# Score masks added by VectorE, softmax sums inverted in packed form and spread by way of DRAM

## What is computed

```python
B, S, D = (2, 512, 512)           # x has shape (2, 512, 512)
NH, NKV = (32, 8); HD = D // NH   # 32 heads of 16, 8 key/value groups of 4 heads each
q, k, v = x @ wq, x @ wk, x @ wv
scores = einsum('bihd,bjhd->bhij', q, k) * HD ** -0.5
scores = where(causal, scores, finfo.min)
attn = softmax(scores, axis=-1)
out = einsum('bhij,bjhd->bihd', attn, v).reshape(b, s, NH * HD) @ wo
```

## Time and profile before

| | us |
|---|---|
| median of 3 runs | 952.16 |
| range of the runs | 950.35 to 952.4 |
| the profiled execution | 952.0 |
| its span in the profile | 950.1 |
| attention stage in it | about 84 to 289 |

### The profile page before, as it was taken

How to read it: one execution, slowest core, us unless ns; L and a number is a source line. 1 busy time by engine, 2 the same in 40 slices (tenths; PEclk the granted TensorE clock), 3 DMA queues, 4 the chain that set the end, 5 groups by cost and what they waited for, 6 DMA issues and landing times.

```text
span 950.1 us, 13799 instructions
## 1 busy us (share of the span) xinstructions
PE 877.9 (92%) x5224; PEld 693.3 (73%) x5224; DVE 693.6 (73%) x892; ACT 533.1 (56%) x707; POOL 189.5 (20%) x197
## 2 busy tenths in 40 slices
PE   2799999999988889898999999999988999999996
PEld 1567667666667668686888888788866888888885
DVE  3835698888888768778677777587887866667842
ACT  3313667657654434486666657477727766666830
POOL 3002555666557213300000000000040000000004
PEclk9798999999898999999999999999999999999998
DMA  9588565655535103105233333133312333332202
GB/s 309 171 243 152 67 109 69 113 101 66 103 78 179 34 12 105 51 22 147 83 106 103 102 99 113 46 105 95 111 45 67 111 104 97 99 101 67 67 1 89
DMA packets 40610, 93.59 MB, mean 99 GB/s; under 512 B 7000, under 2 KB 10072, under 8 KB 40544
## 3 DMA queue, kind: packets, MB, share of 16 engines
q1 hardware_dynamic: 36416, 87.35, 36.6%
q10 hardware_dynamic: 4128, 5.36, 1.7%
HBM read 77.98 MB, written 2.11 MB: 84 GB/s over the span
## 4 chain that ended last, share of the span: by engine, by line
PE 75%; DVE 9%; issue 5%; POOL 4%; ACT 3%; DMA 2%; SPq 1%; POOLq 0%; DVEq 0%; ACTq 0%
PE PS L1509 15%; PE PS L1510 14%; PE PS L1511 14%; PE PS L1815 5%; PE PS L1814 5%; PE PS L1813 5%; PE PS L1607 4%; PE PS L1639 2%; PE PS L1622 2%; DVE MX L1295 2%; POOL QS L731 2%; DMA WM<-in_WM 1%; POOL X L715 1%; PE PS L1531 1%; DVE ACC L1157 1%
## 5 line engine op out<-in xcount | busy, mean ns | idle before, releaser
L837 ACT ACTIVATE PL<-CODE 128x1024 f32<-128x1024 int32 x200 | 201.9, 1057 | 60.3 <-DVE ACC L1157 55.7
L1509 PE MATMUL PS<-HH,WRH 128*128 128x512 f32 x448 | 176.7, 394 | 11.2 <-DVE HL L1116 4.7
L1510 PE MATMUL PS<-HH,WRL 128*128 128x512 f32 x448 | 175.6, 392 | 0.0
L1511 PE MATMUL PS<-HL,WRH 128*128 128x512 f32 x448 | 175.6, 392 | 0.0
L715 POOL TENSOR_TENSOR X<-X,SCR 128x512 f32<-128x512 f32 x32 | 42.6, 1343 | 560.2 <-DVE SCR L1142 560.1
L1157 DVE SCALAR_TENSOR_TENSOR ACC<-PL,ACC 128x1024 f32<-128x1024 f32 x100 | 123.1, 1231 | 8.4
L879 ACT ACTIVATE PT<-PS 128x512 f32<-128x512 f32 x160 | 85.5, 602 | 67.3 <-PE PS L1622 45.1
L1295 DVE TENSOR_REDUCE MX<-PS 128x2 f32<-128x256 f32 (+3 forms) x128 | 100.5, 820 | 29.4 <-PE PS L1609 14.8
L1509 PEld LDWEIGHTS PS<-HH,WRH 128*128 128x128 f32 x448 | 84.9, 189 | 31.2 <-issue 6.3
L731 POOL TENSOR_TENSOR QS<-ident,MX 64x256 fp32r<-64x256 f32 x128 | 93.6, 732 | 66.6 <-DVE MX L1295 60.0
L1511 PEld LDWEIGHTS PS<-HL,WRH 128*128 128x128 f32 x448 | 84.8, 189 | 18.0
(11 more groups left out here) (225 smaller groups left out, 1528.2 us busy)
## 6 DMA issues: line engine op xcount, KB each, us to landing
CODE<-in_CODES SPq DMA_DIRECT2D x50, 512.0 KB, 3.5
SCALE<-in_SCALES SPq DMA_DIRECT2D x100, 256.0 KB, 4.0
WM<-in_WM SPq DMA_DIRECT2D x12, 1024.0 KB, 5.9
QS<-FH SPq DMA_DIRECT2D x32, 128.0 KB, 4.1
QS<-FL SPq DMA_DIRECT2D x32, 128.0 KB, 5.1
X<-in_X ACTq DMA_DIRECT2D x2, 1024.0 KB, 12.3
GAB<-gates SPq DMA_DIRECT2D x4, 512.0 KB, 3.8
out_x<-X ACTq DMA_DIRECT2D x8, 256.0 KB, 2.0
```

The lines of the kernel that those rows point to most:

```text
L837: nc.scalar.activation(PL[:, n % 3], CODE[:, p % 2], ACT.Prelu, scale=scale, bias=bias, alpha=alpha).then_inc(s_plane, 1)
L1509: nc.tensor.matmul(dst, lh, rh, start=start and k == 0, stop=False)
L1510: nc.tensor.matmul(dst, ll, rh, start=False, stop=False)
L1511: ins = nc.tensor.matmul(dst, lh, rl, start=False, stop=stop and k == KC - 1)
```

## The change

- `scores(n)` no longer adds the mask by a product. DVE reads each head's scores and a mask CMASK (three blocks of zeros and the triangular block, so that its last (ic + 1) x 128 columns fit every unit), adds them, writes the sum back over the scores, and takes the maximum in the same instruction: four `tensor_tensor_reduce` a unit in place of two `reduce_max`. The transposed scores keep their mask product. POOL writes CMASK once before unit 0.
- For pairs 0 to 5 the shuffle and the two reciprocals are gone. SP packs the sums of a pair (two DMAs, from 4 rows of 512 to 64 rows of 32 each) into RC, DVE inverts RC (128x32) at u = 7, SP stores it to DRAM (two DMAs) with odd and even group exchanged, and spreads it over the 128 partitions of DENS (one DMA, 2 KB each). The division comes at u = 16 for pairs 0 to 4, at unit 61 for pair 5; before, it came at u = 9. Pair 6 is swapped, inverted and divided as before, in units 61 to 63; pair 7 after the loop as before.
- The packs of pair c stand on SP's queue ahead of stack 2c + 5, the stores ahead of stack 2c + 6 (pair 5's behind stack 15), the spread behind stack 2c + 6 (pair 5's behind stack 15).
- `step_at` uses slots 0, 1, 5 of eight units in place of 2, 4, 6. `ROUND_AT` moves pair 5 from unit 60 to 62.

```diff
--- before.py
+++ after.py
@@ -78,12 +78,16 @@
 
 LOW_RANK_AT = [(0, KC - 1), (1, 1), (1, KC - 1)]
 PAIRS = GROUPS // 2
-ROUND_AT = {41: 0, 46: 1, 49: 2, 54: 3, 58: 4, 60: 5, 63: 6}
+ROUND_AT = {41: 0, 46: 1, 49: 2, 54: 3, 58: 4, 62: 5, 63: 6}
 SPLIT_AT = {46: 0, 51: 1, 54: 2, 59: 3}
 SWAP = list(range(HD, 2 * HD)) + list(range(HD))
 
 
 STEPS = len(CAPS) + 1
+
+
+PACK_AT = {2 * pair + 5: pair for pair in range(B * PAIRS - 2)}
+SPREAD_AT = {min(2 * pair + 6, B * GROUPS - 1): pair for pair in range(B * PAIRS - 2)}
 
 
 SECOND_AT = 2
@@ -115,7 +119,7 @@
 
 def step_at(n):
 
-    slots = (2, 4, 6)
+    slots = (0, 1, 5)
     if not 0 <= n < B * GROUPS * TB or n % 8 not in slots:
         return None
     return divmod(n // 8 * len(slots) + slots.index(n % 8), STEPS)
@@ -247,6 +251,8 @@
         MR = sb("MR", [P, D], F32)
         gab0 = at[0]
         GAB = sb("GAB", [P, B, D], F32)
+        CMASK = sb("CMASK", [P, TB * P], F32, gab0)
+        RC = sb("RC", [P, S // HD], F32, gab0 + 4 * TB * P)
         MCOL = sb("MCOL", [P, 2, 4, KC, B], F32)
         ident = sb("ident", [P, P], F32)
         maskR = sb("maskR", [P, P], F32R)
@@ -359,6 +365,7 @@
         XN = [sb(f"XN{n}", [P, TB, D], F32, R0 + off * K) for n, off in enumerate((40, 40, 40, 40))]
         XM = [sb(f"XM{n}", [P, 2, D], F32, R0 + off * K) for n, off in enumerate((72, 16, 80, 48))]
 
+        INV = nc.dram_tensor("inverses", (REP, 2, S), F32, kind="Internal").ap()
         GD = nc.dram_tensor("gates", (4, B, D), F32, kind="Internal").ap()
 
         PS = ctx.enter_context(nc.psum_tensor("PS", [P, 8, 512], F32))
@@ -432,6 +439,10 @@
         s_pl = sem("projection_weights_split")
         s_ll = sem("lora_weights_split")
         s_gd = sem("gates_stored")
+        s_dn = sem("denominators_packed")
+        s_ri = sem("denominators_inverted")
+        s_rs = sem("inverses_stored")
+        s_rb = sem("inverses_spread")
         s_gab = sem("gates_spread")
         s_sg = sem("silu_ready")
         s_hsh = sem("hidden_rounded")
@@ -535,6 +546,31 @@
                 sp.wait_ge(s_free, J[last_gated(i - 1)] + 1)
             sp.wait_ge(s_gd, 16 * B)
             sp.dma_start(GAB[:], GD[i:i + 1].to_broadcast([P, B, D])).then_inc(s_gab, 16)
+
+        def pack_sums(sp, pair):
+
+            b, c = divmod(pair, PAIRS)
+            sp.wait_ge(s_odd, 2 * pair + 2)
+            if pair:
+                sp.wait_ge(s_rs, 32 * pair)
+            for u in range(2):
+                sp.dma_start(RC[64 * u:64 * u + 64], DEN[HD * u:P:2 * HD, c, b * S:(b + 1) * S]).then_inc(s_dn, 16)
+
+        def store_inverses(sp, pair):
+
+            sp.wait_ge(s_ri, pair + 1)
+            if pair:
+                sp.wait_ge(s_rb, 16 * pair)
+            for u in range(2):
+                sp.dma_start(INV[:, 1 - u], RC[64 * u:64 * u + 64]).then_inc(s_rs, 16)
+
+        def spread_inverses(sp, pair):
+
+            sp.wait_ge(s_rs, 32 * (pair + 1))
+            if pair:
+                sp.wait_ge(s_div, pair)
+            sp.dma_start(DENS[:], INV.rearrange("h u s -> (h u) s").unsqueeze(1).to_broadcast([GROUPS, HD, S])
+                         ).then_inc(s_rb, 16)
 
         def load_stack(sp, n):
 
@@ -621,7 +657,15 @@
                                  ).then_inc(s_wm[n % 3], 16)
 
             for n in range(B * GROUPS):
+                if n in PACK_AT:
+                    pack_sums(sp, PACK_AT[n])
+                if n - 1 in PACK_AT:
+                    store_inverses(sp, PACK_AT[n - 1])
                 load_stack(sp, n)
+                if n == B * GROUPS - 1:
+                    store_inverses(sp, PACK_AT[n])
+                if n in SPREAD_AT:
+                    spread_inverses(sp, SPREAD_AT[n])
                 if n == STACKS:
                     sp.wait_ge(s_mr, 1)
                     for b in range(B):
@@ -674,6 +718,11 @@
             pool.wait_ge(s_free, J["norm", 0, B - 1, KC - 1] + 1)
             for odd in range(2):
                 link(nc.gpsimd.memset(V[:, :, odd::2, 1 - odd, :], 1.0))
+            pool.wait_ge(s_mm, J["modcol", 1, COLS[-1]] + 1)
+            pool.wait_ge(s_const, 16 * 3)
+            link(nc.gpsimd.memset(CMASK[:, 0:(TB - 1) * P], 0.0))
+            nc.gpsimd.tensor_copy(CMASK[:, (TB - 1) * P:], maskB[:]).then_inc(s_ones, 1)
+            pool.wait_ge(s_ones, 3)
             pool.wait_ge(s_mm, J["v", B - 1] + 1)
             for i in range(1, STACKS):
                 link(nc.gpsimd.memset(KN[i][64:P].bitcast(F32), -1.0))
@@ -1226,8 +1275,14 @@
                 cols = slice(half * (S // 2), (half + 1) * (S // 2))
                 link(nc.vector.reciprocal(DENS[:, cols], DENS[:, cols]))
 
+            def invert_packed(pair):
+                dve.wait_ge(s_dn, 32 * (pair + 1))
+                nc.vector.reciprocal(RC[:], RC[:]).then_inc(s_ri, 1)
+
             def divide(pair):
                 b, c = divmod(pair, PAIRS)
+                if pair < B * PAIRS - 2:
+                    dve.wait_ge(s_rb, 16 * (pair + 1))
                 cols = slice(b * S, (b + 1) * S)
                 nc.vector.tensor_tensor(NUM[:, c, cols], NUM[:, c, cols], DENS[:], ALU.mult).then_inc(s_div, 1)
                 dve.wait_ge(s_div, pair + 1)
@@ -1292,21 +1347,30 @@
                     if n >= 2:
                         dve.wait_ge(s_dg, 2 * (n - 1))
                     w = (n % TB + 1) * P
-                    nc.vector.reduce_max(MX[:, n % 2, 2 * pair:2 * pair + 2], PS[:, 2 * pair:2 * pair + 2, 0:w], AX_X
-                                         ).then_inc(s_mx, 1)
+                    if n == 0:
+                        dve.wait_ge(s_ones, 3)
+                    for h in (2 * pair, 2 * pair + 1):
+                        ins = nc.vector.tensor_tensor_reduce(PS[:, h, 0:w], PS[:, h, 0:w], CMASK[:, TB * P - w:], 1.0,
+                                                             MASKED, ALU.add, ALU.max, MX[:, n % 2, h:h + 1])
+                    ins.then_inc(s_mx, 1)
                 if step_at(n) and step_at(n)[1] < STEPS - 1:
                     curve_sum(*step_at(n))
                 if n == TB - 1:
                     gate_values()
                 if pair_at(n, 4) is not None:
                     copy_odd(pair_at(n, 4))
-                if pair_at(n, 5) is not None:
-                    swap_sums(pair_at(n, 5))
-                for half, unit in enumerate((5, 6) if n >= 60 else (7, 8)):
-                    if pair_at(n, unit) is not None:
-                        invert(half)
-                if pair_at(n, 7 if n >= 60 else 9) is not None:
-                    divide(pair_at(n, 7 if n >= 60 else 9))
+                if pair_at(n, 7) in PACK_AT.values():
+                    invert_packed(pair_at(n, 7))
+                if pair_at(n, 16) in range(B * PAIRS - 3):
+                    divide(pair_at(n, 16))
+                if n == B * GROUPS * TB - 3:
+                    divide(B * PAIRS - 3)
+                    swap_sums(B * PAIRS - 2)
+                    invert(0)
+                if n == B * GROUPS * TB - 2:
+                    invert(1)
+                if n == B * GROUPS * TB - 1:
+                    divide(B * PAIRS - 2)
                 if n in SPLIT_AT:
                     split_heads(SPLIT_AT[n])
 
@@ -1604,10 +1668,8 @@
                     if n >= 1:
                         pe.wait_ge(s_mx, 2 * (n - 1) + half + 1)
                     for h in (2 * half, 2 * half + 1):
-                        nc.tensor.matmul(PS[:, h, 0:(ic + 1) * P], QS[:, q % STACKS, h, ic * P:(ic + 1) * P],
+                        ins = nc.tensor.matmul(PS[:, h, 0:(ic + 1) * P], QS[:, q % STACKS, h, ic * P:(ic + 1) * P],
                                          KS[:, q % STACKS, 0:(ic + 1) * P], start=True, stop=True)
-                        ins = nc.tensor.matmul(PS[:, h, ic * P:(ic + 1) * P], identR, maskR[:], start=False, stop=True,
-                                               skip_group_check=True)
                     ins.then_inc(s_s, 1)
 
             def transposed(n):
```

## The result

Median of the change 979.11 us (973.26 to 980.22, 4 runs), beside it the kernel before at 952.28: ratio 1.0271, 95% interval 1.0226 to 1.0316. The profiled execution took 978.4 us, its span is 976.6. So the change costs 26 us where 14 were forecast. The busy times on the page after, which answer to the earlier trace rows: PE has 11.0 us less, DVE 1.6 less, and still the kernel is slower.

The account below looks back on a forecast made before the run. In the attention stage PE and DVE were both nearly full and waited for each other. From 952.0 us, adding 0 (PE against DVE), 7.4 (moved decode steps), 3.4 (clock) and 3.0 (SP's queue) gave 966 us; range 944 to 984.

Parts of the forecast that it names:

- its own case: Whole kernel: the forecast of 966 us, 960 to 974, given a chance of 0.42.
- dear maxima: Rival on DVE: each delivered maximum costs 0.177 instead of 0.07 us, half of 27 us exposed, 980 us; chance 0.17.
- Term B: Moved decode steps: ACT waits for codes of piece 4 (4.5 us) and longer for piece 5; +7.4 us, bounds +4 and +12.
- term C: Granted clock: PE slows after the new wait for piece 4's codes; +3.4 us, bounds 0 and 7.
- Term A: PE against DVE in attention: PE loses 18.6 us of masks, DVE gains 3.6 net; taken as 0, bounds -18.6 and +15.
- Term D: SP's queue: five more DMAs for each of six pairs use up its idle time; +3 us, bounds 0 and +18.
- Faster: Rival in attention: cheap maxima, fewer reciprocals and PE's relief win; the stage gains 8 us at most, 944 us; chance 0.20.
- Queue and clock hold: Rival: SP's queue absorbs its added DMAs and the clock holds; 959 us (954 to 960); chance 0.17.
- the signs named beforehand: Profile after: two ACT code waits of 4 to 8 us, lower clock, maxima 0.533 plus 0.14 to 0.2 us, groups near 11.4.

Follow-up runs that it names:

- e6: Kernel before with only the codes of pieces 2 to 5 issued ahead of the stack loads: 949.9 us, ratio 0.9964.
- e7: Kernel before with packed softmax sums and early codes; masks stay on PE, slots 2, 4, 6: 950.5 us, ratio 0.9981.
- e8: The whole change, but with decode slots 2, 4, 6 and early codes: 951.9 us, ratio 1.0019.
- e2: The change with its new slots, but the codes of pieces 2 to 5 issued ahead of the stack loads: 960.8 us, ratio 1.0098.
- e4: Kernel before with only the masks of the first scores moved from PE to DVE: 959.0 us, ratio 1.0072.
- e1: The change with the decode slots put back to 2, 4, 6, nothing else different: 959.5 us, ratio 1.0082.
- e3: Kernel before with only the decode slots moved to 0, 1, 5: 979.0 us, ratio 1.0284.
- e9: Kernel before with decode slots 0, 1, 5 and early codes: 964.9 us, ratio 1.0123.
- e12: Kernel before with packed sums, decode slots 0, 1, 5 and early codes; masks stay on PE: 963.4 us, ratio 1.0140.
- e10: Kernel before without the mask products in the first scores and nothing in their place: 947.2 us, ratio 0.9962.
- e5: Kernel before with only the softmax sums packed; masks on PE, slots 2, 4, 6, late codes: 957.3 us, ratio 1.0053.
- e11: Kernel before with packed sums, early codes, old slots and no mask in the first scores: 951.3 us, ratio 0.9997.

## Why the prediction was right or wrong

**The direction and the wide range (944 to 984) held; the forecast was 13 us too low, and the 960 to 974 given for its own case were missed by 5.** That the time lies inside the range is in part luck: the range reached so far up for dear maxima, whose 980 is next to the 979 measured, and the maxima were not dear.

One chain of runs in which each step changes one thing adds up to the 25.8 us (each step to some 3 us, the last to some 5): from the kernel before to e6 (early codes) -3.4, to e7 (sums) +1.6, to e8 (masks) +3.6, to e2 (slots) +7.5, to the change (late codes) +16.5. So late codes cost 13.1 more than they did before, where B and C had 10.8; the masks 3.6, where A had 0; the sums 1.6, where D had 3; and the place of the slots 7.5, which no term had. This last one is the largest miss. Another order gives other shares: masks 6.9 (e4), sums on top 0.9 (e1 less e4), slots with the codes that they make late 18.0.

**Term B (+7.4) and term C (+3.4): right mechanism, somewhat too small.** The two waits came at exactly the two places named, 6.64 and 8.05 us in place of 4.5 and 4.4 to 5. Without the packed sums they were 4.43 and 3.94 (e3), so the sum behind B holds for the slots alone. The step that failed is that issue and landing were taken at the times of the trace before. Piece 4's codes were to be issued 0.43 us after ACT's last exponential; behind a spread, a pack and eleven us of stack it became 2.5, and 2.5 + 4.16 is the 6.64. Piece 5's came 1.1 us after it, as forecast, but took 7.0 us from issue to use instead of 4.05, right behind a spread. The clock was counted with one new wait, at 3.4 us. Counted in the same way, 10 us x (1 - granted clock), the four windows shown give 1.3 + 3.8 + 4.1 + 2.7 = 11.9 us, of which the kernel before already had 3.4: an upper bound, since PE stood idle for part of them. The runs measure both terms together: early codes take 16.5 us from the change and 3.4 from the kernel before, and the 13.1 between them stand against 10.8.

**What the prediction did not have: where the slots lie.** It followed the moved steps for their codes only. That 5 and 8 = 5 + 3 are both slots, so that curves and a fold meet behind the copy of the even group in one unit of ACT, could be read from `ride(n + 3)` and `step_at`. It costs 7.5 us in the change and 15.1 on the kernel before (e9 less e6). In one group 6.5 us of it are shown for the masked kernels (e2, e8) and 5.1 for e12; the rest stays open.

**Term A (0): too small by 3 to 7 us.** Masks cost 6.9 us alone (e4), 3.6 where the sums are packed and codes early (e8 less e7). The maxima's price was near: heads of 512 elements follow each other every 0.65 us on DVE (119.35, 120.00, 120.64 in its timeline), heads of 128 every 0.25, which is 1.04 ns an element, so 0.115 to 0.12 us over the 0.533 and 0.133 of their elements. The plain reduction goes at the same pace, from 686 ns at 512 elements to the 1217 at 1024 of the earlier trace rows (groups by shape before, 84 to 284 us):

```profile
L1295 DVE TENSOR_REDUCE MX<-PS 128x2 f32<-128x512 f32 x32 | 20.7, 686 | 2.3 <-PE PS L1609 1.9
```

Per unit that is 4 x 0.115 - 2 x 0.07 = 0.32 us more, 20.5 us in all against the 26.9 predicted. What failed is the exchange: PE's 18.6 us were set against DVE's net of 3.6 and taken as no loss and no gain. By e10, PE's relief is worth 3.6, so the 20.5 us of DVE's masks in e4 cost about 10.5 of exposed time (an estimate: 6.9 + 3.6), and they cost it where the packed sums (23 us less) do not pay: these are saved in three units of eight, the maxima are dearer in every one. The 11.45 us of the earlier trace rows isn't the shortest group either: by DVE's first maxima six of the fifteen before took less, the shortest 10.7.

The Trainium skill (VectorE: DVE Perf Modes, section on two Vector instructions with no wait) has an op with an accumulator output as two instructions. The trace after agrees: 256 rows of READ_ACCUMULATOR, 141 ns each. The time between heads shows, though, that only part of that is added, since the next head's instruction starts with it (both at 120.00).

**Term D (+3): near in size, and the harm came by another way.** The sums alone cost 5.0 us (e5), and 1.6 with early codes (e7 less e6): 3.4 of the 5.0 come by the late codes, in part by their slower landing behind a spread, which no term had. That the queue would hardly wait any more was wrong for the change, where it waited 29 us (16.6 before), nearly all of it for PE's transposed scores; it was right for e11.

**Rivals.** *Faster* fell: PE's relief gave 3.6 us, not 18.6, and even with neither late codes nor new slots the change is 1.8 us slower. *Dear maxima* fell by their price. *Queue and clock hold* fell by both. Of the signs named beforehand, those of B, C and the maxima (0.53 plus 0.12; groups of 11.4 us, 97.12 to 108.51) came as written. The reciprocal of 128x32 took 0.348 us where 0.35 was read off its length.

**Not tried.** Early codes with no mask in the first scores and the sums as before would join the edits of e6 and e10, which gained 3.4 and 3.6 us apart; e11 tells only that with packed sums nothing is gained. Nor was the late load of codes tried with the spread moved behind it, or a third set of slots, in which the fold and the curves of the next piece stand apart. The maxima over unmasked scores need scores whose range can't drive all exponentials of a row to zero.

## What to carry to other kernels

When a step is moved between units, go through every engine's order for what it then stands beside (here `n` and `n + 3` on ACT) and through every load that it needs: its load must move with it. A load that one engine's whole list stands behind belongs ahead of bulk loads on a shared queue; moving four of them gave 3.4 us to the kernel before, and 16.5 to the change. Work taken from an engine at 84 to 92% of a stretch gives back little if it was not in the units where that engine ends last: 18.6 us from PE gave 3.6, and 23 from DVE none once the DMAs that they took were paid.

## What the runs showed of the hardware

- A masked add with maximum, read from and written back to PSUM, goes at the pace of the plain maximum, 1.04 ns an element: from head to head 0.65 us at 512 elements and 0.25 at 128 (after), 0.115 to 0.12 of it beside the elements.
- A load of 512 KB (codes of a piece) landed in 3.6 to 4.2 us in 22 of 24 cases in the kernels without spreads, and in 5.0 to 7.2 us in all eleven cases in which a DMA of 256 KB to 128 partitions (the spread) had been started on the same queue within 2.1 us before it (after: 7.2 and 6.9; e5: 5.4 and 6.6). No run tells why.
- The granted clock in the ten us in which a wait of ACT for codes ended, or in the next ten, fell to 0.79 behind 2.1 us (before), 0.83 behind 1.68 (e4) and 2.34 (e10), 0.78 and 0.66 behind 4.43 and 3.94 (e3), 0.66 and 0.71 behind 1.57 and 6.46 (e1), 0.71 behind 7.23 (e5), 0.62 and 0.59 behind 6.64 and 8.05 (after). So it fell behind every one, but not in proportion to the wait. In e2, where no such wait is left, it was 0.90 or more from 200 to 290 us. The lowest was 0.53, in e11, where DVE waited 5.85 us for a pack.
